# Attention edges of a graph kernel: one tile of 32 copied row by row by SyncE and ScalarE instead of gathered by GpSimd

## What is computed

```
def gat_layer(h, src, dst, W, al, ar, b):
    feat = (h @ W).reshape(n, H, F)                     # 4 heads of 64
    el = jnp.sum(feat * al[None], axis=-1)
    er = jnp.sum(feat * ar[None], axis=-1)
    e = jax.nn.leaky_relu(el[src] + er[dst], NEG_SLOPE)
    m = jax.ops.segment_max(e, dst, num_segments=n)
    ex = jnp.exp(e - m[dst])
    denom = jax.ops.segment_sum(ex, dst, num_segments=n)
    msg = feat[src] * (ex / denom[dst])[:, :, None]
    out = jax.ops.segment_sum(msg, dst, num_segments=n) + b
    return jax.nn.elu(out)
```

## Time and profile before

| | us |
|---|---|
| median of 3 runs | 7234.83 (7234.73 to 7235.01) |
| profiled execution, its own time | 7229.16 |
| profiled execution, its span | 7227.0 |
| first attention layer's edges | about 2807 to 4795 |
| second attention layer's edges | about 5079 to 7067 |

### The profile page before, as it was taken

One profiled execution on the slowest core, in us unless ns is written; L12 is line 12 of the kernel. 1 busy time (PEld: TensorE's weight loads), 2 busy tenths in 40 slices (PEclk: granted clock), 3 DMA queues, 4 the chain that ended last, 5 costly groups with the idle time before them and its releaser, 6 DMA issues. The chain is left out here.

```text
span 7227.0 us, 61561 instructions
## 1 busy us (share of the span) xinstructions
PE 2303.9 (32%) x10543; PEld 1547.9 (21%) x10543; DVE 5489.4 (76%) x9603; ACT 2205.4 (31%) x5460; POOL 5224.6 (72%) x5323
## 2 busy tenths in 40 slices
PE   4688888888888573000000000026000000000000
PEld 3455555555555463000000000014000000000000
DVE  7799999999999576666666666674567676666678
ACT  2688888888888341000000000011000000000001
POOL 4677777777776536777777777767777777777775
PEclk8899999999999797555555555558555555555555
DMA  7666676666766567676767676754566676767677
GB/s 229 191 204 203 204 204 204 203 205 202 206 203 194 140 162 184 208 222 208 223 208 223 207 224 207 223 162 102 176 211 219 211 221 209 221 208 223 209 228 235
DMA packets 821966, 1467.60 MB, mean 203 GB/s; under 512 B 215801, under 2 KB 552574, under 8 KB 821372
## 3 DMA queue, kind: packets, MB, share of 16 engines
q0 software_dynamic: 250192, 671.13, 34.9%
q1 hardware_dynamic: 571692, 795.57, 32.3%
HBM read 754.20 MB, written 713.36 MB: 203 GB/s over the span
## 5 line engine op out<-in xcount | busy, mean ns | idle before, releaser
L1781 POOL DMA_INDIRECT gb_g<-table,ix_g x3126 | 2974.8, 952 | 954.8 <-issue 950.3
L666 POOL DMA_INDIRECT gb<-table,ix x1563 | 1615.8, 1034 | 495.1 <-issue 471.2
L1887 DVE SCALAR_TENSOR_TENSOR gb_g<-gb_g,same_g,wv 128x256 f32<-128x256 f32 x3020 | 1447.9, 479 | 94.2
L1051 PE MATMUL pm<-ident,tl 128*4 128x128 f32 x2 | 0.7, 373 | 4013.3 <-DMA tl<-sums 4013.3
L1814 ACT ACTIVATE ww<-ee 128x132 f32<-128x132 f32 (+5 forms) x106 | 29.2, 276 | 3646.1 <-DVE ee L1865 3646.1
L1875 DVE TENSOR_TENSOR wv<-gb_g,ww 128x1024 f32<-128x1024 f32 (+1 forms) x784 | 955.1, 1218 | 0.0
L697 PE MATMUL po<-msg,sel 128*128 128x256 f32 x3144 | 857.4, 420 | 145.5 <-DVE msg L809 141.1
L1051 PEld LDWEIGHTS pm<-ident,tl 128*4 128x4 f32 x2 | 0.2, 82 | 4014.2 <-DMA tl<-sums 4014.2
L1857 DVE TENSOR_TENSOR ee<-gb_g,held 128x128 f32<-128x128 f32 (+5 forms) x106 | 38.5, 363 | 1073.9 <-DMA gb_g<-table,ix_g 1073.9
L697 PEld LDWEIGHTS po<-msg,sel 128*128 128x128 f32 x3144 | 613.5, 205 | 380.7 <-DVE msg L809 240.9
L689 PE MATMUL pt<-m,r 64*128 64x256 f32 x3136 | 462.1, 413 | 228.3 <-DVE msg L850 225.1
(11 more groups left out here) (291 smaller groups left out, 4354.0 us busy)
## 6 DMA issues: line engine op xcount, KB each, us to landing
sums<-gb_g SPq DMA_DIRECT2D x780, 528.0 KB, 3.5
sums<-ost SPq DMA_DIRECT2D x393, 512.0 KB, 3.2
gb_g<-table,ix_g POOLq DMA_INDIRECT x3126, 3.1
gb<-table,ix POOLq DMA_INDIRECT x1563
table<-f SPq DMA_DIRECT2D x48, 520.0 KB, 7.4
x<-in_x SPq DMA_DIRECT2D x50, 256.0 KB, 4.1
at<-in_rbf SPq DMA_DIRECT2D x100, 128.0 KB
hT_d<-hT SPq DMA_DIRECT2D x49, 256.0 KB, 3.7
```

The lines of the kernel that those rows point to most:

```text
L666: eng.indirect_dma_start(out=gb[:, g, j, :, :].rearrange("p a c -> p (a c)"), out_offset=None, in_=q.table0[:, :], in_offset=bass.Indirect ...
L1781: eng.indirect_dma_start(out=gb[:, p, j, 0:FR], out_offset=None, in_=q.table1[:, :], in_offset=bass.IndirectOffsetOnAxis(ap=ix[:, p, j:j + ...
L1887: ins = eng.scalar_tensor_tensor(rows[:, t0 + t, 0:D], row, same[:, t:t + 1], wv[k % 2][:, j, :], ALU.mult, ALU.add)
```

## The change

One tile of each group, number 26, is taken from the gathers (`TAKEN`). GpSimd issues 31 gathers a group. The 128 rows of the taken tile are copied by 128 transfers of a single row each: rows 0 to 63 by SyncE, rows 64 to 127 by ScalarE. Their places in the table come from registers. A new input `src_taken` holds the source nodes of the taken tiles; it is loaded once a layer into three partitions of `at_i`, VectorE multiplies it by the row's 1040 bytes, and each sequencer then loads 32 values at a time into registers and issues one transfer for each, out of the table seen as bytes.

Both sequencers copy two groups ahead: in the body of group s for group s+2, after the same conditions as GpSimd's gathers of that group (`free_again`). On SyncE the 64 copies stand at the head of the body, ahead of the index tile and of the eight stores of group s. On ScalarE they stand behind the exponential and the two copies of group s. For groups 0 and 1 both issue all their copies before their loops, on SyncE ahead of the fills of `sums`. VectorE waits for the gathers and for both kinds of copies.

```diff
+TAKEN = ((26,), (26,), (26,))
+MOST = max(len(x) for x in TAKEN)
...
+        at_i = sb(c, f"at_i{n}", [B, SB // B + 1, MOST, P], I32)
...
-        s_g = [Signal(q.sem(nm(f"g{p}")), per=SBT, inc=16) for p in range(B)]
+        s_g = [Signal(q.sem(nm(f"g{p}")), per=SBT - len(TAKEN[p]), inc=16) for p in range(B)]
+        s_rs, s_ra = ([Signal(q.sem(nm(f"{x}{p}")), per=len(TAKEN[p]) * P // 2, inc=16) for p in range(B)] for x in ("rs", "ra"))
+        s_at, s_by = q.sem(nm("at")), q.sem(nm("by"))
...
+        table_bytes = q.table1.rearrange("n f -> (n f)").bitcast(U8)
+        ROW = 4 * FR
+
+        def places(eng, i, p, r0, r1):
+            line = at_i[p:p + 1, :, :, :].rearrange("a i m r -> a (i m r)")
+            _, values = nc.values_load_multi_w_load_instructions(line[:, bass.ds(i * (MOST * P) + r0, r1 - r0)], engines=[eng.engine], min_val=0,
+                                                                 max_val=(N - 1) * ROW, skip_runtime_bounds_check_because="they are places of nodes' rows")
+            return values
+
+        def row(eng, p, r, place, signal):
+            m, r = divmod(r, P)
+            eng.dma_start(gb[r:r + 1, p, TAKEN[p][m], 0:FR].bitcast(U8), table_bytes[bass.ds(place, ROW)].unsqueeze(0)).then_inc(signal.sem, 16)
+
+        def free_again(eng, s, i, p):
+            if p == B - 1:
+                eng.wait_ge(s_held, H)
+            eng.wait_ge(s_st[p].sem, s_st[p].at(i, back=1))
+            eng.nop(nofuse=True)
+            eng.wait_ge(s_sum.sem, s_sum.at(s, 1, back=2))
+            eng.nop(nofuse=True)
...
             @block.sync
...
+                mine = [[(m * P + r, min(m * P + r + 32, m * P + P // 2)) for m in range(len(x)) for r in range(0, P // 2, 32)] for x in TAKEN]
+                parts = [[(r0, r1, r) for r0, r1 in x for r in range(r0, r1, 8)] for x in mine]
+                wanted = []
+
+                def copies(i, p, k):
+                    r0, r1, r = parts[p][k]
+                    if r == r0:
+                        wanted[:] = places(eng, i, p, r0, r1)
+                    for x in range(r, min(r + 8, r1)):
+                        row(eng, p, x, wanted[x - r0], s_rs[p])
+
                 def body(s, i, p, more):
+                    i2, p2 = i + (p + 2) // B, (p + 2) % B
+                    free_again(eng, s + 2, i2, p2)
+                    for k in range(len(parts[p2])):
+                        copies(i2, p2, k)
                     if more:
                         eng.wait_ge(s_g[p].sem, s_g[p].at(i))
                         eng.nop(nofuse=True)
                         indices(i * B + (p + B), p)
                     eng.wait_ge(s_seg.sem, s_seg.at(s))
+                    eng.nop(nofuse=True)
...
+                eng.dma_start(at_i[:, :, :, :], a["src_taken"]).then_inc(s_at, 16)
+                eng.wait_ge(s_by, 1)
+                for p in range(B - 1):
+                    for k in range(len(parts[p])):
+                        copies(0, p, k)
...
             @block.gpsimd
...
                     for j in range(SBT):
-                        rows(j, p, s_g[p].sem)
+                        if j not in TAKEN[p]:
+                            rows(j, p, s_g[p].sem)
...
             @block.scalar
...
+                def copies(i, p):
+                    for m in range(len(TAKEN[p])):
+                        for r0 in range(m * P + P // 2, m * P + P, 32):
+                            for x, place in enumerate(places(eng, i, p, r0, r0 + 32)):
+                                row(eng, p, r0 + x, place, s_ra[p])
+
+                def ahead(s, i, p):
+                    i2, p2 = i + (p + 2) // B, (p + 2) % B
+                    free_again(eng, s + 2, i2, p2)
+                    copies(i2, p2)
+
...
+                eng.wait_ge(s_by, 1)
+                for p in range(B - 1):
+                    copies(0, p)
                 with eng.Fori(0, LOOPS) as i:
                     for p in range(B):
                         body(i * B + p, p, 0, SBT)
+                        ahead(i * B + p, i, p)
...
             @block.vector
...
-                    eng.wait_ge(*arrived)
+                    for signal in arrived:
+                        eng.wait_ge(*signal)
...
+                eng.wait_ge(s_at, 16)
+                eng.tensor_scalar(at_i[:, :, :, :], at_i[:, :, :, :], ROW, None, ALU.mult).then_inc(s_by, 1)
```

More of the change, by code:

```diff
@@ L5 @@
 from concourse import mybir
-F32, I32, BF16 = mybir.dt.float32, mybir.dt.int32, mybir.dt.bfloat16
+F32, I32, BF16, U8 = mybir.dt.float32, mybir.dt.int32, mybir.dt.bfloat16, mybir.dt.uint8
 ALU, ACT = mybir.AluOpType, mybir.ActivationFunctionType
@@ L1806, in _ @@
                     for j in range(t0, t1):
-                        rows(j, s % B, s_ge[x])
+                        if j not in TAKEN[s % B]:
+                            rows(j, s % B, s_ge[x])
             @block.scalar
@@ L1823, in _ @@
                         body(i * B + p, p, 0, SBT)
+                        ahead(i * B + p, i, p)
                 for p in range(B - 1):
                     body(LOOPS * B + p, p, 0, SBT)
+                    ahead(LOOPS * B + p, LOOPS, p)
                 for x, (s, t0, t1) in enumerate(ENDS):
@@ L1920, in whole @@
                     body(s, p, 0, SBT, s * SBT, [y[:, bass.ds(s * (H * W), H * W)] for y in (q.seg_add, q.seg_back, q.seg_mul)],
-                         (s_g[p].sem, s_g[p].at(i)), s_sum.at(s, 0), gb[:, (p - 1) % B, SBT - 1, 0:D], SBT)
+                         [(y[p].sem, y[p].at(i)) for y in (s_g, s_rs, s_ra)], s_sum.at(s, 0), gb[:, (p - 1) % B, SBT - 1, 0:D], SBT)
                 with eng.Fori(0, LOOPS) as i:
@@ L1930, in _ @@
                     p = s % B
+                    held_by = [t for t in TAKEN[p] if t0 <= t < t1]
                     body(SB - 2 + x, p, t0, t1, s * SBT + t0, [y[:, :] for y in end_masks[x]],
-                         (s_ge[x], 16 * (t1 - t0)), summed(x),
+                         [(s_ge[x], 16 * (t1 - t0 - len(held_by)))] + [(y[p].sem, y[p].at(s // B)) for y in (s_rs, s_ra) if held_by], summed(x),
                          gb[:, p, t0 - 1, 0:D] if t0 else gb[:, (p - 1) % B, SBT - 1, 0:D], ENDS[x - 1][2] - ENDS[x - 1][1] if x else SBT)
@@ L1953 @@
         "src_chunks": _np.concatenate([srcp[:EC].reshape(P, CE), _np.zeros((P, CH - CE + 2 * SBT), src.dtype)], axis=1),
+        "src_taken": _np.stack([_np.concatenate([srcp[:EC].reshape(P, CE), _np.zeros((P, (SB + 2) * SBT - CE), src.dtype)], axis=1).T.reshape(SB + 2, SBT, P)[p::3, list(x + x[:1] * (MOST - len(x)))]
+                                for p, x in enumerate(TAKEN)]),
         "dst_rows": dstp.reshape(T, P),
```

## The result

The changed kernel takes 7802.4 us, the median of four runs (7795.3 to 7804.1), where the kernel before took 7234.8 (7230.5 to 7235.0): 1.078 times as long, with an interval of 1.077 to 1.080, or 568 us more. The profiled execution took 7804.1 us, its span is 7802.4. The forecast was 8100, in a range of 7120 to 8800. The direction and the mechanism came out as said; the sum was 298 us too high.

A forecast was written before the change was run, and what follows sets the result against it. GpSimd's gather issuing was the bound; SyncE's chain of copies, burst and landing would replace it at 48 us a group. 432 us a layer, 864 for two, added to 7234.8 gave 8100 us, range 7120 to 8800.

The forecast's parts named there:

- What bounds the kernel: Attention-edge gathers: GpSimd's issuing paces a group at 40.07 us; after the change SyncE's chain does, chance 0.63.
- The copy: One single-row transfer on SyncE or ScalarE: 0.504 us, between 0.42 and 0.63; 64 of them 32.3 us a group.
- The DMA instruction: Issue part of one single-row copy: taken 0.31 us, between ends 0.287 and 0.354.
- The address: Register work for one copy's place: taken 0.10 us, between 0.067 for a MOVE alone and 0.15 as a store has.
- The register load: Loading one copy's place into a register: taken 0.056 us, as 1.8 us for 32; ends 0.029 and 0.085.
- The burst: Group's eight stores on SyncE, leaving together behind the copies: 15 us from first issue to last landing, 13.6 to 21.
- The period: One group on SyncE: copies 32.3, index tile and waits 0.8, burst to landing 15, so 48 us; range 41.3 to 58.
- the one-off costs: Layer start and end: 65 us of copies for groups 0 and 1, SyncE's loop from 2923, ScalarE's last block 33.
- What would show it: Profile signs: 48 us groups, 64 issues then eight stores, POOL waiting some 9 us, last store landing over 10 us late.
- It fits: Rival: SyncE's chain stays under GpSimd's 38.75 us a group, copies at most 0.36 to 0.38 us; 7129 us, chance 0.15.
- Loads one at a time: Rival: each register value on SyncE and ScalarE loaded singly, 0.77 us a copy, 65 us a group, 9660 us; chance 0.07.
- slow issues in pairs: Rival: copies issued back to back or by both sequencers slow down, 0.81 us each, 68 us a group, 9940; chance 0.12.

The follow-up runs named there:

- g1 to g4: Changed kernel with gathers replaced by plain transfers, four variants in order and place of the single-row copies: 8224.6, 7827.2, 7534.5 and 7903.9 us.
- g1: Changed kernel with gathers replaced by five plain transfers of consecutive rows a group; both sequencers copy, ahead of SyncE's stores: 8224.6 us, 42.5 a group.
- g4: As g1, but ScalarE issues no copies, a plain transfer of GpSimd brings its rows; SyncE's 64 stay ahead of its stores: 7903.9 us, 39.5 a group.
- h2: As g1, but ScalarE issues only 32 of its 64 copies, a plain transfer of GpSimd brings the rest: 7249.6 us, 39.6 a group.

## Why the prediction came out as it did

**What bounds the kernel** held. The chain on SyncE's ring, closed by the landing of its own burst, is the new pace; g1 to g4 show it with the gathers taken away, and in the changed kernel its pieces, read from the trace, add up to the period.

**The copy, 0.504 forecast, 0.387 measured.** This is the term that was mis-sized, and it is 7 us of a group.
- The DMA instruction: 0.31 taken between L536's 0.287 and an index tile's 0.354; it took 0.225, under both ends. L536 is the first single row behind another kind of transfer, and here, too, the first of a block takes 0.327; the rows behind it are cheaper.
- The address: 0.10 was the mean of a MOVE alone and a MOVE with a FUSED_REGOPS. It is the MOVE alone, as the reasoning on the byte offset had it.
- The register load: 0.056 a value, from an index tile's landing, against 0.064 measured, 2.04 us for 32.
64 copies are then 24.8 us where 32.3 were forecast; the range's low end, 27, was too high. For fetching more code the forecast had nothing to 1 us, from no row; the copies' block leaves at most 0.5 us for it (25.3 from the first load's start to the last issue's end).

**The burst, 15 forecast, 18 to 19 measured,** errs the other way by 3.7 us. In pieces: alone it lands after 12.4 (h2), where 11.6 + 2 = 13.6 was worked out from the earlier trace rows. The gathers beside it add what is left of the difference, about 3, where 1 to 2 stood; since the copies are shorter, GpSimd is still at its gathers for most of the burst and not for 6 us of it. The straggling engine adds 3, and nothing in the sum stood for it. The prediction said that the single rows' bytes are nothing; they are, but their number on one engine is not.

**The period** follows: 25.5 + 1.0 + 18.7 = 45.2, against 48. The two errors have opposite signs, and by that luck the forecast was nearer than its terms. From the period, 46 x 45.2 - 1776 = 303 us a layer, less 10 because the shorter copies let SyncE's loop start at 2913 and not 2923, and less 7 for ScalarE's last block: 2 x 286 = 572. Measured are 568. So the one-off costs and the way from a group to the whole were right.

**What would show it.** The block of 64 issues, the burst, and a last store that lands over 10 us after its issue came as said (first stores 4.7 us, last 10 to 11). GpSimd's wait for the landing is 7 us and not 9: its own group is 38.75 in 45.2 as before in 48. The stores are not 0.65 us apart but up to 1.6, as their issue takes 0.9 to 1.3 us once three are out. Wrong was the place of VectorE's wait. It was to grow ahead of L1857, and was found behind it, at ScalarE's exponential. The forecast had ScalarE's chain at 40 under SyncE's 48 and left out that both wait for the same landing: ScalarE's copies begin with SyncE's and end with them, and the exponential comes only then. It looks like the bound and is not: in g4 ScalarE has no copies, the exponential follows at once, and the group still takes 39.5.

**The rivals.** *It fits* wanted copies of 0.36; they were 0.387, and the burst, with the straggler and the gathers beside it, took back 3.7 of the 7 us that the copies had saved. With a burst of 18.7 the copies would have had to take 0.30; with a burst of 12.4, as in h2, the ring is 39.6 and still just over GpSimd's 38.75. The rival's own time, 7129, leaves out a term of the forecast's sum, ScalarE's last block behind the landing of group 45: with it, and the loop starting at 2904, it is some 7190. The price it named from L536, 0.354, was still closer than the one that I took. *Loads one at a time* (0.77 a copy) and *slow issues in pairs* (0.81) fell: 0.387, with 64 places in two loads. The Trainium skill, "Runtime: NRT & Kernel Launch", Instruction fetch mechanics, has 200 ns for each register, on a page that speaks of loads from device memory; out of SBUF 64 were measured. For its lock on the generator, "Perfetto Trace Analysis", DMA Instruction — HWDGE, g1 has both engines' instructions over the same 23 us:

```profile
L1756 SPq DMA_DIRECT2D gb_g<-table x64: 224/225/327, 4113.7 to 4136.7; - x64
...
L1756 ACTq DMA_DIRECT2D gb_g<-table x64: 213/228/472, 4113.8 to 4137.1; - x64
```

In h2 ScalarE stops after 10.5 us and SyncE's 64 take 23.1, the same, and in g4, where ScalarE issues nothing, the median of SyncE's is 225 too. Two sequencers that issue single rows at once didn't hold each other up.

## What to carry to other kernels

Before work goes ahead of a queue's stores, ask who waits for the landing of those stores: if it is the same queue, directly or over a freed buffer, the issue time and the landing no longer overlap but add up. Count transfers by DMA engine and not by bytes: many single rows can fill one engine while fifteen are idle, and a wide transfer behind them lands when that one does. And an engine that waits longest in the profile may only be passing on a wait; take its work away before you call it the bound.

## What the runs showed of the hardware that was not expected

- Single-row transfers from both sequencers, one each 0.36 us from either, filled one DMA engine (6.4% of sixteen, 0.18 us a row with nothing beside them) and left it 3 to 3.8 us behind at the end of the next burst; three quarters as many left nothing.
- A load of 32 registers from SBUF takes 2.04 us, beside GpSimd's gathers too, and 4.4 while a burst of stores is carried out.
- In a burst of 0.5 MB stores, the first three are issued in 0.35 to 0.38 us each, the later ones in 0.9 to 1.3: the issue itself waits.
- A chip can be in a condition in which SyncE and ScalarE take about 0.7 us for many of their instructions, a register MOVE as well as a transfer, in stretches in which gathers are carried out. The kernel before loses a fifth by it (8620 to 8670 us against 7235), the changed kernel two fifths (10985 against 7802). In a stage without gathers (g1 to g4) it didn't show.
